# Moving the causal mask multiplies of a fused attention and feed-forward kernel from GpSimd to VectorE

## What is computed

```python
def polymax(x):            # X_INT=-100, Y_INT=1, POWER=2, DIVISOR=1000
    lin  = where((x >= -100) & (x <= 0), -0.01 * x + 1, 0)
    poly = where(x > 0, x ** 2 + 1, 0)
    return (poly + lin) / 1000
qkv = layernorm(x) @ W_attn
att = einsum('bhid,bhjd->bhij', q, k) / 8
att = where(causal, att, -inf)
x = x + (polymax(att) @ v) @ W_proj
h = gelu((layernorm(x) @ U1) @ V1 + b1)
x = x + (h @ U2) @ V2 + b2
```

## Time and profile before

| | us |
|---|---|
| median of two runs | 2324.98 (2322.62 to 2327.34) |
| the profiled execution | 2322.57 |
| its span, slowest core (3) | 2321.0 |
| spans of the eight cores | 2306.6 to 2321.0 |
| busy PE, DVE, ACT, POOL | 1313.6, 1227.7, 762.2, 471.9 |
| POOL, in its 516 instructions | 512 of them are L730 and L735 |

### The profile page before, as it was taken

The page is one execution under the profiler, slowest core; times in us unless marked ns, Lnnn a source line. Parts: engine busy times, 40 slices in busy tenths (PEclk is TensorE's granted clock), DMA queues, the critical chain, the costliest instruction groups (busy, mean ns, idle before and its releaser), DMA issues.

```text
span 2321.0 us, 23460 instructions; the slowest of 8 cores (2306.6 to 2321.0 us)
## 1 busy us (share of the span) xinstructions
PE 1313.6 (57%) x6880; PEld 473.6 (20%) x6880; DVE 1227.7 (53%) x1659; ACT 762.2 (33%) x1074; POOL 471.9 (20%) x516
## 2 busy tenths in 40 slices
PE   3422657574455557776646376445555360458876
PEld 0000223331111111111112133111111120013332
DVE  3667333345576669999963233557766122353332
ACT  1100000004465567777750000446555000113333
POOL 0000000018856550000000000885665000000000
PEclk8655779895556567777778699555666685558888
DMA  5444121100000000000011200000000425000000
GB/s 152 142 156 151 55 73 36 37 1 1 1 1 1 1 1 1 1 1 1 1 37 37 73 1 1 1 1 1 1 1 2 139 95 163 0 0 37 37 37 37
DMA packets 37340, 87.74 MB, mean 38 GB/s; under 512 B 1889, under 2 KB 7266, under 8 KB 37218
## 3 DMA queue, kind: packets, MB, share of 16 engines
q1 hardware_dynamic: 30498, 75.75, 10.0%
q10 hardware_dynamic: 6720, 10.49, 1.5%
HBM read 77.85 MB, written 8.39 MB: 37 GB/s over the span
## 4 chain that ended last, share of the span: by engine, by line
PE 40%; issue 18%; DVE 15%; DMA 11%; POOL 10%; ACT 5%; DVEq 0%; SPq 0%; POOLq 0%; ACTq 0%
PE ps L757 6%; POOL poolD L735 6%; DVE poolD L721 5%; DMA poolD<-W_attn 5%; PE ps L688 5%; POOL poolD L730 4%; PE ps L1055 3%; PE ps L868 3%; ACT poolD L708 3%; PE ps L1036 3%; PE ps L592 3%; PE ps L853 2%; PE ps L612 2%; PE ps L634 2%; PE ps L952 2%
## 5 line engine op out<-in xcount | busy, mean ns | idle before, releaser
L708 ACT ACTIVATE poolD<-ps 128x1024 bf16<-128x1024 f32 (+3 forms) x640 | 561.7, 902 | 1023.3 <-PE ps L688 786.2
L721 DVE SCALAR_TENSOR_TENSOR poolD<-poolD 128x1024 bf16<-128x1024 bf16 (+3 forms) x640 | 703.6, 1154 | 176.3 <-PE ps L765 105.8
L757 PE MATMUL ps<-poolD,poolA 128*64 128x512 bf16 (+3 forms) x1280 | 316.1, 479 | 398.3 <-POOL poolD L735 280.4
L730 POOL TENSOR_TENSOR poolD<-poolD,sb_masksb 128x256 bf16<-128x256 bf16 x256 | 266.3, 1040 | 1320.7 <-ACT poolD L713 1206.4
L688 PE MATMUL ps<-poolB,poolA 64*128 64x512 bf16 (+3 forms) x1280 | 288.7, 478 | 33.1 <-ACT poolD L708 16.0
L735 POOL TENSOR_TENSOR poolD<-poolD,sb_masksb 128x256 bf16<-128x256 bf16 x256 | 222.9, 871 | 2.4 <-ACT poolD L708 2.4
L757 PEld LDWEIGHTS ps<-poolD,poolA 128*64 128x64 bf16 x1280 | 94.5, 120 | 593.0 <-issue 593.0
L1047 ACT ACTIVATE poolC<-ps,sb_b1s 128x512 bf16<-128x512 f32 x128 | 88.1, 689 | 128.0 <-PE ps L1036 128.0
L713 ACT ACTIVATE poolD<-ps,consts 128x256 bf16<-128x256 f32 x256 | 124.6, 487 | 2.6 <-POOL poolD L730 2.6
L688 PEld LDWEIGHTS ps<-poolB,poolA 64*128 64x128 bf16 x1280 | 65.2, 103 | 243.1 <-issue 242.0
L952 PE MATMUL ps<-poolC,poolD 128*128 128x512 bf16 x256 | 63.8, 415 | 59.2 <-DVE poolD L902 38.9
(11 more groups left out here) (100 smaller groups left out, 1159.6 us busy)
## 6 DMA issues: line engine op xcount, KB each, us to landing
poolD<-x_t SPq DMA_DIRECT2D x8, 2048.0 KB, 10.0
poolA<-x_t SPq DMA_DIRECT2D x8, 2048.0 KB, 10.1
poolD<-W_attn SPq DMA_DIRECT2D x12, 1024.0 KB, 4.9
poolD<-W_attn SPq DMA_DIRECT2D x16, 512.0 KB, 3.6
poolC<-x_own_t SPq DMA_DIRECT2D x4, 2048.0 KB, 8.0
y<-poolC SPq DMA_DIRECT2D x4, 2048.0 KB, 6.6
poolD<-W_proj SPq DMA_DIRECT2D x8, 512.0 KB, 3.6
poolD<-U ACTq DMA_DIRECT2D x5, 512.0 KB, 4.6
```

What stands on the lines that cost most here:

```text
L708: e.activation(o, i, AF.Relu), inc="S")
L721: e.scalar_tensor_tensor(o, i, 0.01, i, ALU.add, ALU.mult),
L730: e.tensor_mul(o, z, m), inc="P")
L757: e.matmul(o, l, r, skip_group_check=True, start=st, stop=True, tile_position=tp),
```

## The change

The two mask multiplies of a masked tile are issued on DVE instead of POOL. Their operands and the formula stay as they were. They count on V instead of P, so ACT waits for V where it waited for P before it overwrites `zb`, and PE waits for one value of V ahead of a masked AV. The number that ACT waits for before it overwrites `eb` (`e_rel`) is read from V's count after the multiplies, so for a masked tile it now includes them. POOL's waits for S and T fall away, because DVE has made the same waits ahead of L721.

```diff
-                            b.wait("scalar", "P", zw_rel[sb])
+                            b.wait("scalar", "V", zw_rel[sb])
...
                         if masked:
                             midx = ktg % 2
-                            b.wait("gpsimd", "S", s_rel[sb])
-                            b.wait("gpsimd", "T", g_rel[sb])
-                            zw_rel[sb] = b.op("gpsimd", lambda e, o=zmb[:, sb, :, :],
+                            zw_rel[sb] = b.op("vector", lambda e, o=zmb[:, sb, :, :],
                                               z=zb[:, sb, :, :], m=masksb[:, midx, :, :]:
-                                              e.tensor_mul(o, z, m), inc="P")
-                            b.wait("gpsimd", "V", gcnt[idx])
-                            mcnt[idx] = b.op("gpsimd",
+                                              e.tensor_mul(o, z, m), inc="V")
+                            b.wait("vector", "V", gcnt[idx])
+                            mcnt[idx] = b.op("vector",
                                              lambda e, o=gb[:, 2 * sb:2 * sb + 2, 0:128],
                                              m=masksb[:, midx, :, :]:
-                                             e.tensor_mul(o, o, m), inc="P")
+                                             e.tensor_mul(o, o, m), inc="V")
                         e_rel[sb] = b.cnt["V"]
...
-                        b.wait("tensor", "V", gcnt[idx])
-                        if is_m(idx):
-                            b.wait("tensor", "P", mcnt[idx])
+                        b.wait("tensor", "V", mcnt[idx] if is_m(idx) else gcnt[idx])
```

## The result

The changed kernel takes 2148.81 us (median of 11 runs, 2143.78 to 2173.58), the kernel before 2327.02 us (10 runs). The ratio is 0.922, with a 95% interval of 0.919 to 0.926: 7.8% faster. In some executions the cores of one die get a lower clock and take longer; the medians take these in, the ratios leave them out. The forecast was 2143 us, with 2122 to 2213 as its range.

A forecast was written before the change was run, and what follows sets the result against it. POOL and DVE taking turns on one shared SBUF port bound the masked heads; 16 A heads 5.61 us and 16 B heads 5.73 us shorter, 181 us together, gave 2143 us, range 2122 to 2213.

The forecast's parts named there:

- The bound: In masked heads POOL and DVE take turns on one shared SBUF port; an A head takes 17.59 us, a B head 26.43.
- L721: DVE operation in each tile: 1.135, 0.868, 0.602, 0.335 us start to start by width; eight masked ones sum to 5.88 us.
- The multiplies: Mask multiplies moved to DVE go in pairs of elements, 0.202 us start to start; sixteen cost 3.23 us a head.
- The rival of one element at a time: Each DVE mask multiply costs 0.33 us and not 0.20: 67 us more, 2210 us; chance 0.09.
- Whole durations: Rival: each DVE operation in the masked chain costs its whole duration, 2.0 us a head, 64 us: 2207 us; chance 0.12.
- The waits: The second multiply's wait for L721 and ACT's Relu waiting for both multiplies were each costed at nothing.
- The second multiply's own wait: On DVE, waiting for L721 with the first multiply between costs nothing; with nothing between, 0.03 us behind the end.
- The ring: Rival: PE, ACT and DVE obstruct each other by 0.55 us a masked tile, 141 us: 2284 us; within-2% losses, chance 0.05.
- The sum: Sixteen A heads save 5.61 us each and sixteen B heads 5.73, together 181 us, for 2143 us.
- The clock that the forecast allowed for as a low side: A higher granted PE clock in masked tiles shortens each head's fill and drain, at most 18 us: 2125 us.

The follow-up runs named there:

- The runs with fewer multiplies: Against the changed kernel: both multiplies left out, 2104.49 us; PE masks scores, z's multiply kept, 2106.02 us; additionally ACT masks z in odd key tiles, 2095.29 us.

## Why the prediction was right

*The bound.* POOL and DVE in turns on one port: that the turns are taken and what they cost is shown, by the two runs in which POOL works for nobody. That a head of the kernel before was bound by them is read from its rows: POOL's 14.70 us of work in an A head and its 2.89 us of standing still make up the 17.59. What the forecast did not know is the price of a turn. The expectations of the experiments used the whole span of the multiply, 0.66 us, where the runs show mostly 0.28 to 0.47 of DVE: 0.41 on average with POOL's extra multiply, 0.43 with g on POOL, 0.37 with z there. In the forecast's own sum this does not appear, since all turns went away; it made my expectation of the run with g on POOL 31 us too high at its lower end.

*L721.* Forecast from end points at 1024 and 128 elements: 1.135, 0.868, 0.602, 0.335. The trace after: 1.15 or 1.13, 0.86, 0.60, 0.33.

*The multiplies.* 0.202 us, taken from a copy of half as many elements because L420 showed that pairs are possible. The trace has 0.20, the third multiply 0.197. The rival of one element at a time stood on 0.33; the float32 mask gives 0.34 and 61 us, so it would have been a real loss of gain had it held.

*Whole durations.* The rows overlap by 0.08 us in this chain of three kinds too. The Trainium skill's sentence that the next operation does not start until the pipe is empty (VectorE: DVE Perf Modes, "The DRAIN you can't avoid") is not what these rows show. The forecast gave it without its exception, for the same paragraph of the Trainium skill adds that "A next op that is not held starts earlier", and with that these rows agree, by the 0.08 us. The run with the third multiply, 51 us and not 74, decides for the rows.

*The waits.* ACT's longer wait cost nothing, shown by taking it away. The second multiply's own wait cost nothing with one operation between, as forecast; but the price next to its writer, 0.19 us and not 0.12, was mis-sized, and only the order of the two multiplies kept it out of the sum.

*The ring.* The forecast's margins of 0.8 to 1.2 us a tile held: inside a head DVE has hardly any idle time. The runs with fewer multiplies show how near the next bound is in an A head. Taking 1.6 us out of DVE's part of it, at the price of 2.3 us more on PE, gave 0.23. In a B head the same edit gave all of its 1.6 us.

*The sum.* Forecast 11.98 and 20.70 us a head. Undisturbed heads take 12.00 and 20.71 (633.72 to 654.43 is one). The stretches' means are 12.09 and 20.85, so 16 x 5.50 + 16 x 5.58 = 177 us, 4 less than the 181 forecast. What makes the difference are single stalls of about 0.3 us on DVE, such as this one:

```profile
525.63 0.29 DVE L728 TENSOR_TENSOR poolD<-poolD,sb_masksb 128x256 bf16<-128x256 bf16 x1
526.20 0.29 DVE L733 TENSOR_TENSOR poolD<-poolD,sb_masksb 128x256 bf16<-128x256 bf16 x1 [0.27 <-DVE poolD L728]
```

Here the operation stood ready, and 0.27 us passed. The traces point at a cause. Each of the eight cores has eight or nine such stalls of over 0.2 us in its masked tiles, at the same places of DVE's list on every core. Counting waits as well, these places are multiples of 128 instructions apart, to within two. An 8 KB packet of kind "instruction" on queue q14 starts 0.5 to 1.0 us behind each. So they seem to come with the loading of DVE's own program; no run took that away, so it is not shown. The spans differ by 2321.0 - 2147.1 = 173.9 us, so 3 us more were lost outside the masked stages. The medians of the result differ by 178.2. The clock that the forecast allowed for as a low side stayed away in A heads (0.50 as before). It rose in B heads from 0.62 to 0.66, and that gave nothing: from QK to the first L721 a B head takes 1.92 us before and after.

## What to carry to other kernels

An engine that is "half idle" is no place to offload to when it shares a port with the engine it relieves: here a POOL multiply that read SBUF took about 0.4 us from DVE where the two met, and DVE does the same multiply in 0.20. In a chain on one engine count strides from start to start, not durations, and put something between an operation and the one that waits for it (0.19 us each time here). Before taking more work off the bound, ask how far the next one is, and what the replacement costs there: 1.6 us less on DVE, paid with 2.3 us more on PE, shortened an A head by 0.23.

## What the runs showed of the hardware beyond what was expected

- A POOL multiply of 128 x 256 bf16 takes 0.66 us alone and lengthens one DVE operation with two SBUF inputs where they meet, mostly by 0.28 to 0.47 us. POOL's fill of the same tile, 0.31 us, lengthens none.
- An operation on DVE that waits for the one right ahead of it started 0.10 us behind that one's end. Without a wait it starts 0.08 to 0.09 us before the end.
- The granted clock of the B stretches rose from 0.66 to 0.85 when PE got two more short matmuls in each masked tile; that of the A stretches stayed at 0.50.
- The run with z on POOL is 21 us slower than the one with g there. Its trace has the own wait in every masked tile (46 us), which the other does not have, and turns of 94 us against 87; the other pays 0.5 us at the end of each head and waits for POOL inside some B heads.
- Not settled: whether the stalls of about 0.3 us on DVE with everything ready are the loading of its program, and why the stages without masks differ by a few us between profiles of kernels that are the same there.
